# Splitting the routed experts' weights early, through DRAM, and building the one-hot tables in eight pieces

## The reference, cut to what matters

```python
x = x + L0_ffn(L0_cond(x, ...))        # attention (16 heads, cosine), then relu^2 MLP 256->1024->256, then a 5-step spiking count
x = x + L1_ffn(L1_cond(x, ...))        # attention (16 heads), then a transformer block with a mixture of experts
# inside L1_ffn, for the normed token t:
probs  = softmax(t @ Wr.T)             # 8 experts; the best 2 by probs + bias are taken
routed = sum_k w_k * (silu(t @ eW1[e_k].T) * (t @ eW3[e_k].T)) @ eW2[e_k].T
shared = (silu(t @ sW1.T) * (t @ sW3.T)) @ sW2.T
```

## Time and profile before

| what | value |
|---|---|
| median of three runs | 1526.59 us (1524.34 to 1528.87) |
| the profiled execution, its span | 1527.73 us, 1526.0 us |
| PE busy | 1349.5 us (88%) |
| DVE, ACT, POOL busy | 1127.1 (74%), 893.8 (59%), 795.6 us (52%) |
| mean granted TensorE clock | 0.957 of full |

### The profile page before, as it was taken

The page is one execution under the profiler, slowest core; times in us unless marked ns, Lnnn a source line. Parts: engine busy times, 40 slices in busy tenths (PEclk is TensorE's granted clock), DMA queues, the critical chain, the costliest instruction groups (busy, mean ns, idle before and its releaser), DMA issues.

```text
span 1526.0 us, 43298 instructions
## 1 busy us (share of the span) xinstructions
PE 1349.5 (88%) x15534; PEld 1178.9 (77%) x15535; DVE 1127.1 (74%) x2218; ACT 893.8 (59%) x2229; POOL 795.6 (52%) x838
## 2 busy tenths in 40 slices
PE   1889999999759999979999999768998867999993
PEld 0778988889648999868888888547787756888883
DVE  4488888888844556689999999748886797545457
ACT  1457767667527666746665666437786544545556
POOL 1256656665505545555555555358884023777740
PEclk9899999999979999999999999979997989999997
DMA  7210000000011000000000000110003203233318
GB/s 203 33 36 8 9 8 8 10 8 9 33 30 53 1 0 0 1 9 9 9 7 9 9 9 8 26 48 15 14 14 111 74 1 121 93 101 99 96 43 331
DMA packets 82391, 65.09 MB, mean 43 GB/s; under 512 B 50734, under 2 KB 76081, under 8 KB 81202
## 3 DMA queue, kind: packets, MB, share of 16 engines
q1 hardware_dynamic: 75314, 44.98, 10.3%
q0 software_dynamic: 6912, 17.84, 3.7%
HBM read 39.18 MB, written 18.35 MB: 38 GB/s over the span
## 4 chain that ended last, share of the span: by engine, by line
PE 75%; DVE 10%; issue 6%; ACT 5%; POOL 2%; SPq 1%; DMA 1%; DVEq 0%; ACTq 0%; POOLq 0%
PE psW L1968 12%; PE psQ L1889 12%; PE psQ L2261 8%; PE psW L2240 4%; PE psS L1950 4%; PE psS L1993 4%; PE psT L1926 3%; PE psQ L2062 3%; PE psW L2050 3%; PE psM L2050 3%; PE psS L2062 3%; PE psM L1937 2%; PE psT L2229 1%; PE psM L1907 1%; PE psT L2248 1%
## 5 line engine op out<-in xcount | busy, mean ns | idle before, releaser
L732 POOL TENSOR_TENSOR pn<-ex,rden 128x1024 f32<-128x1024 f32 x64 | 144.0, 2250 | 245.3 <-PE psT L1926 240.7
L1889 PEld LDWEIGHTS psQ<-xT,wq 128*128 128x128 f32 x1536 | 201.1, 200 | 46.0 <-issue 24.1
L1968 PE MATMUL psW<-wout,oT 128*128 128x256 f32 x1536 | 210.3, 292 | 16.4 <-ACT oT L963 14.4
L1889 PE MATMUL psQ<-xT,wq 128*128 128x256 f32 x1536 | 220.9, 297 | 1.5 <-ACT cur L1044 1.5
L1968 PEld LDWEIGHTS psW<-wout,oT 128*128 128x128 f32 x1536 | 195.3, 194 | 29.3 <-ACT oT L963 24.0
L2261 PE MATMUL psQ<-W,exT 128*128 (+1 forms) x624 | 173.8, 414 | 0.0
L777 POOL TENSOR_TENSOR hT<-hf,hT 128x512 fp32r<-128x512 f32 x64 | 84.4, 1318 | 99.9 <-ACT hT L1040 99.9
L2261 PEld LDWEIGHTS psQ<-W,exT 128*128 128x128 f32 x624 | 112.2, 193 | 19.2
L2240 PE MATMUL psW<-W,ehT 128*128 (+1 forms) x624 | 103.4, 303 | 8.3 <-DVE ehT L1803 8.2
L1347 DVE SCALAR_TENSOR_TENSOR oT<-psS,nvcol,oT 128x512 fp32r<-128x512 f32 x128 | 89.7, 740 | 23.8 <-ACT oT L963 23.2
L1320 DVE TENSOR_TENSOR ex<-ex,m 128x1040 f32<-128x1040 f32 x64 | 103.6, 1619 | 2.2
(11 more groups left out here) (310 smaller groups left out, 3477.3 us busy)
## 6 DMA issues: line engine op xcount, KB each, us to landing
both<-results SPq DMA_DIRECT2D x8, 1024.0 KB, 13.3
raw_w<-W SPq DMA_DIRECT2D x27, 256.0 KB, 4.2
vv<-vp SPq DMA_DIRECT2D x256, 16.0 KB, 1.8
xf<-xf_all SPq DMA_DIRECT2D x4, 1024.0 KB
out<-X SPq DMA_DIRECT2D x8, 512.0 KB, 5.0
X<-x SPq DMA_DIRECT2D x1, 3584.0 KB, 14.3
raw_q<-Wq SPq DMA_DIRECT2D x2, 1024.0 KB, 6.0
bvv<-v_all SPq DMA_DIRECT2D x128, 16.0 KB, 1.8
```

The source lines that it names most:

```text
L732: nc.gpsimd.tensor_tensor(pn[:], ex[t % 2][:, :, 0:S], rden[:].unsqueeze(2).to_broadcast([P, H, S]), ALU.mult).then_inc(sem("t_pn"), 1)
L1889: mm = nc.tensor.matmul(psQ[:, cc, h * QT:h * QT + QT], wq[w][:, k, c * P:c * P + P], xT[g % 2][u][:, k, :], start=(k == 0 and j == 0), st ...
L1968: mm = nc.tensor.matmul(psW[:, 0:D], oT[u][:, c, :], wout[w][:, c, :], start=(u == 0 and c == 0 and w == 0), stop=(u == 1 and c == CH - 1))
```

## The change

The weights of the eight routed experts are no longer split in the routing stage. In each of the eight groups of the feed-forward, one expert is loaded into a small buffer, its three pieces are split at f = 1, 3 and 5 (the hi copy on ScalarE, the lo on VectorE, one pair of buffers for both), and SyncE stores hi and lo into a DRAM tensor. Each expert later comes into its slot by one load of 1.57 MB. Only the shared expert is still split in place, at steps -4 to -2. The one-hot tables are made in eight pieces of 8 columns through two buffers each, so they take one slot instead of four; TensorE multiplies a piece in each of steps 13 to 20. Ranking, scan with tile ends, and places move to steps 9, 10 and 11, the tables' product ends at step 20, and the index tables move from step 20 to 21. Three semaphores are merged into others.

```diff
-PROBS, CHOICE, RANK, SCAN, ENDS, PLACES, HOT, SLOTS, TABLES = 5, 6, 10, 11, 12, 13, 14, 19, 20
+PROBS, CHOICE, RANK, SCAN, PLACES, HOT, SLOTS, TABLES = 5, 6, 9, 10, 11, 12, 19, 21
+PIECES = 8
-SPLIT_STEP = ([-4, -3, -2] + [0, 1, 2] + [3, 4, 5] + [10, 10, 10] + [SLOTS] * 3 + [21] * 4 + [22] * 4 + [23] * 4)
+SPLIT_STEP = (-4, -3, -2)
+PRE = 3 * E
+PRE_F = (1, 3, 5)
...
+        pre_raw = sb("ffn_work", "pre_raw", [P, EW], F32)
+        pre_w = [sb("ffn_work", f"pre_w{i}", [P, 2 * D], F32R) for i in range(2)]
+        w_dram = nc.dram_tensor("split_w", (E, P, 2, EW), F32, kind="Internal").ap()
...   SyncE, after the fside loads of layer 1 and before its attention
+            sp.dma_start(g2col[:], a["g2"].rearrange("(k p) -> p k", p=P), ...).then_inc(sem("e_first"), 16)
+            for g in range(E):
+                reach(sp, sem("e_wlo"), 3 * g)
+                load_expert(g + 1, pre_raw[:])
+                for part in range(3):
+                    sp.wait_ge(sem("e_wlo"), 3 * g + part + 1)
+                    third = slice(part * 2 * D, part * 2 * D + 2 * D)
+                    for w in range(2):
+                        sp.dma_start(w_dram[g, :, w, third], pre_w[w][:].bitcast(F32)).then_inc(sem("w_stored"), 16)
...   SyncE, later
+            load_expert(0, raw_w[:, SHARED_SLOT, 1, :])
+            sp.wait_ge(sem("w_stored"), 32 * PRE)
+            load_split(1)
...                                            # at the end of the block: load_split(2)
-            for p in (3, EP - 1):
-                load_expert(p, (p + 1) % EP, sem("e_rest"))
-            sp.wait_ge(sem("r_ranked"), 2)
-            sp.wait_ge(sem("r_given"), 3)
-            for p in range(4, EP - 1):
-                load_expert(p, p + 1, sem("e_last"))
+            for p in (3, 5, 6, 7, 8):
+                load_split(p)
+            sp.wait_ge(sem("r_ranked"), 1 + PIECES)
+            load_split(4)
...   ScalarE, in ffn() after ffn_hi() of f = 1, 3, 5
+            def presplit_hi(g, part):
+                act.wait_ge(sem("e_first"), 48 * g + 64)
+                reach(act, sem("w_stored"), 96 * g + 32 * part)
+                nc.scalar.activation(pre_w[0][:], pre_raw[:, part * 2 * D:part * 2 * D + 2 * D], ACT.Copy, scale=...).then_inc(sem("e_whi"), 1)
...   VectorE, in ffn() at f = 1, 3, 5
+            def presplit_lo(g, part):
+                dve.wait_ge(sem("e_whi"), 3 * g + part + 1)
+                ...pre_w[1] = raw * gain - pre_w[0]....then_inc(sem("e_wlo"), 1)
...   VectorE, in first_half()
+                if HOT < i <= HOT + PIECES:
+                    one_hot_rows(i - HOT - 1)
+                if HOT <= i < HOT + PIECES:
+                    one_hot_tiles(i - HOT)
...   ScalarE, in first_half()
+                if HOT <= i < HOT + PIECES:
+                    c = i - HOT
+                    act.wait_ge(sem("r_hot"), c + 1)
+                    nc.scalar.activation(hot_part[c % 2][:], hot_tile[c % 2][:], ACT.Copy, scale=iota_part[:, 0:1]).then_inc(sem("r_part"), 1)
...   TensorE, in first_half()
-                elif i == SLOTS:
-                    pe.wait_ge(sem("r_hots"), 4 + 2 + 1)
+                elif HOT < i <= HOT + PIECES:
+                    c = i - HOT - 1
+                    for ready in ("r_hots", "r_part", "r_number"):
+                        pe.wait_ge(sem(ready), c + 1)
                     ... 16 of the 128 matmuls each time
...   TensorE, the first routed up product (t == FIRST)
-                        pe.wait_ge(sem("e_wlo"), 3 * EP if t else 3)
+                        pe.wait_ge(sem("e_last"), 16 * E)
```

More of the change, by code:

```diff
@@ L62 @@
 WHOLE = 1.5 * 2.0 ** 23
-ORDER = (SHARED_SLOT, 2, 3, 4, 0, 5, 6, 7, 8)
 NEG = -1e30
@@ L400, in build @@
         hot_at = w_at + 5 * 12 * K
-        hot_row = nc.alloc_sbuf_tensor_at("hot_row", [P, TOP_K * TILES, P], BF16, offset=hot_at)
-        hot_tile, hot_part, hot_number = (nc.alloc_sbuf_tensor_at(f"hot_{n}", [P, TOP_K * TILES, ROUTED], BF16, offset=hot_at + 16 * K + 9216 * i)
-                                          for i, n in enumerate(("tile", "part", "number")))
+        region("hot", 12 * K, at=hot_at)
+        HQ = TOP_K * TILES // PIECES
+        hot_row = [sb("hot", f"hot_row{i}", [P, HQ, P], BF16) for i in range(2)]
+        hot_tile, hot_part, hot_number = ([sb("hot", f"hot_{n}{i}", [P, HQ, ROUTED], BF16) for i in range(2)] for n in ("tile", "part", "number"))
         n_tiles = sb("route", "n_tiles", [P, E], F32)
@@ L420, in build @@
         idx = [sb("tile", f"idx{i}", [P, 1], I32) for i in range(BUFS)]
-        by_end = nc.alloc_sbuf_tensor_at("by_end", [1, ROUTED, E], F32, offset=hot_at + 16 * K + 9216 * 3)
+        by_end = nc.alloc_sbuf_tensor_at("by_end", [1, ROUTED, E], F32, offset=place["bias"][0] - 4 * K)
         slot_f = [sb("route", f"slot_f{i}", [1, ROUTED], F32) for i in range(2)]
@@ L859, in store_result @@
                                              oob_is_err=False).then_inc(sem(f"e_stored{m}"), 16)
-            pool.wait_ge(sem("r_hot"), 1)
-            nc.gpsimd.tensor_tensor(hot_number[:], hot_tile[:], number[:].unsqueeze(2).to_broadcast([P, TOP_K * TILES, ROUTED]),
-                                    ALU.mult).then_inc(sem("r_hots"), 1)
+            for c in range(PIECES):
+                pool.wait_ge(sem("r_hot"), c + 1)
+                nc.gpsimd.tensor_tensor(hot_number[c % 2][:], hot_tile[c % 2][:],
+                                        number[:, c * HQ:c * HQ + HQ].unsqueeze(2).to_broadcast([P, HQ, ROUTED]), ALU.mult).then_inc(sem("r_number"), 1)
             pool.wait_ge(sem("xf_stored"), 16 * 5)
@@ L1051, in ffn @@
                     ffn_hi(FC * g + f, f % 2)
+                    if f in PRE_F:
+                        presplit_hi(g, PRE_F.index(f))
                     if last and f == 2:
@@ L1518, in ffn @@
                         ffn_normalise(g + 1)
+                    if f in PRE_F:
+                        presplit_lo(g, PRE_F.index(f))
                     if last and f == 4:
@@ L1621, in _, with split_shared @@
             dve.wait_ge(sem("xf_stored"), 16)
-            def split_expert(n, part):
-                slot = ORDER[n]
-                dve.wait_ge(sem("e_whi"), 3 * n + part + 1)
+            def split_shared(part):
+                dve.wait_ge(sem("e_whi"), PRE + part + 1)
                 third = slice(part * 2 * D, part * 2 * D + 2 * D)
-                hi = W[:, slot, 0, third].bitcast(F32)
-                lo, raw = W[:, slot, 1, third], raw_w[:, slot, 1, third]
+                hi = W[:, SHARED_SLOT, 0, third].bitcast(F32)
+                lo, raw = W[:, SHARED_SLOT, 1, third], raw_w[:, SHARED_SLOT, 1, third]
                 if part < KD:
@@ L1830, in first_half @@
                     top_weights()
-                for piece in range(3 * EP):
-                    if SPLIT_STEP[piece] == i:
-                        split_expert(piece // 3, piece % 3)
+                if HOT < i <= HOT + PIECES:
+                    one_hot_rows(i - HOT - 1)
+                if HOT <= i < HOT + PIECES:
+                    one_hot_tiles(i - HOT)
+                if i == SLOTS:
+                    tile_slots()
+                if i in SPLIT_STEP:
+                    split_shared(SPLIT_STEP.index(i))
             def merged(i):
@@ L2273, in first_half @@
                     mm.then_inc(sem("r_ranked"), 1)
-                elif i == SLOTS:
-                    pe.wait_ge(sem("r_hots"), 4 + 2 + 1)
+                elif HOT < i <= HOT + PIECES:
+                    c = i - HOT - 1
+                    for ready in ("r_hots", "r_part", "r_number"):
+                        pe.wait_ge(sem(ready), c + 1)
                     for b, what in enumerate((hot_part, hot_number)):
-                        for q in range(TOP_K * TILES):
-                            mm = nc.tensor.matmul(psS[:, b, 0:ROUTED], hot_row[:, q, :], what[:, q, :], start=(q == 0), stop=(q == TOP_K * TILES - 1))
+                        for q in range(HQ):
+                            mm = nc.tensor.matmul(psS[:, b, 0:ROUTED], hot_row[c % 2][:, q, :], what[c % 2][:, q, :],
+                                                  start=(c == 0 and q == 0), stop=(c == PIECES - 1 and q == HQ - 1))
                     mm.then_inc(sem("r_ranked"), 1)
```

103 lines of the change are left out of this document (48 added, 55 removed).

## The result

The changed kernel took 1532.84 us (median of 11 runs, 1529.61 to 1538.12) beside 1528.19 for the kernel before (11 runs, 1522.67 to 1530.19): 1.0039 times as long, 95% interval 1.0028 to 1.0051. That is slower by 0.39%, little more than the 0.3% that the prediction took for the smallest change one can tell; 1521.1 was forecast. The spans of the two profiled executions, 1532.0 and 1526.0, differ by 6.0 us, and the stages add up to that. A group of the feed-forward runs from its first transposes to those of the next group; `cur` is the tile that ScalarE copies out when the last group is done; the last step is step 103, a tile of the shared expert.

A forecast was written before the change was run, and what follows sets the result against it. TensorE was taken as the bound, with time to gain only where it waits, before the routed tiles. -12.1 + 4.5 + 1.0 + 1.1 = -5.5 took 1527.73 to 1522.2 us, median 1521.1; 8-in-10 range 1512 to 1532.

The forecast's parts named there:

- Last group: Feed-forward's last group: ScalarE has no idle, three copies 2.0 less 0.9 of gaps; cost 1.1 us, bounds 0 and 2.
- rival A: Middle groups: stores' round trip makes ScalarE wait before second and third hi; 15 us, 1536; chance 0.20.
- Start of the feed-forward: First group: ScalarE waits 5.4 us for the first expert load; cost 4.5 with lowered clock, bounds 2.5 and 8.
- Rival B: Feed-forward's start: first weights land late and the clock drops, cost 8 instead of 4.5, 1525; chance 0.12.
- Middle groups: Feed-forward's middle groups: copies and store waits nearly hidden, 0.2 a group; cost 1.0 us in all, bounds 0 and 15.
- Routing stage: Up to step 25: splits go, tables made in pieces at 4.2 us a step; gain 12.1 us, bounds 17 and 3.
- C: Routing stage: pieces pipeline better, 3.2 us a step instead of 4.2; 7.5 us less, 1513.5; chance 0.17.
- D: Steps 13 to 20: each waits for a piece, TensorE at 1.2 GHz, 5.5 us a step; 9 more, 1530; chance 0.05.

The follow-up runs named there:

- after_again: The changed kernel itself, unaltered, measured again: ratio 1.0057 to the kernel before.
- third_part: third_late, with ScalarE multiplying its piece one step later in the routing stage: ratio 0.9955 to the kernel before.
- third_prod: third_part, with TensorE's product of a piece one step later too and index tables at step 22: ratio 0.9908 to the kernel before.
- no_presplit: The changed kernel without the split and its ScalarE and VectorE pieces; raw weights stored in both halves, loads and stores kept: ratio 0.9979 to the kernel before.
- third_late_b: third_late run once more, beside a trace of the kernel before: ratio 0.9930 to the kernel before.
- third_late: Changed kernel; expert 1 loaded before layer 1's weights, last group's first lo before norm_second, expert 8's third piece between last norm's halves: ratio 0.9989 to kernel before.

## Why the prediction was wrong

The prediction's sum came to 1522.2 for the profiled execution; the changed kernel's took 1533.7. Of these 11.5 us the last group makes 9.2, the first 1.4 and the routing stage 1.3; the middle groups give 0.9 back, and 0.5 is the drift of the two stages that the change does not touch.

*The step that failed* is "Last group": cost 1.1, bounds 0 and 2; it measured 10.3 and 6.8 in two traces. It added up only ScalarE's busy time (three copies, 2.0) and took the group's order from the middle groups. Three things were missing. First, the one pair of buffers: the prediction followed "the next hi waits for the last piece's two stores" through a middle group only. In the last group VectorE's lo piece stands behind norm_second, which waits 4.7 us for GpSimd's rstd, and behind two spike counts; that wait cost nothing before, and no row of the prediction shows it; it became a wait of ScalarE and through it of TensorE. Secondly, the third piece stands in front of wout's 1.90 us and relu(6). Moving the first lo piece took 2.0 off (38.1 to 36.1), moving the third piece 3.6 more (36.1 to 32.5), and 1.2 is left, the lateness of relu(6) that was forecast. In all of these a part is not the wait but TensorE's clock behind it. Thirdly, the exclusion of GpSimd by VectorE, with 3.5 more in one of two traces. The prediction used it as a reason for rival A, where it cost nothing, and did not ask for it where the last down product waits for GpSimd. That it is VectorE's chain which holds GpSimd there rests on the overlap of the rows and on the two lengths of one kernel's operations; no run took the chain away alone.

*Start of the feed-forward*: right in mechanism and place, 5.9 and 6.8 in two traces instead of 4.5. Both terms were too small. Counted from the first transposes, relu(2) came 7.3 and 7.4 us later than before, where 6.1 was worked out, mainly because SyncE took 3.8 and 3.6 us to issue the g2 column and the three loads, not 4 times 0.47. Down(2) came 5.2 and 5.3 later instead of 4.0. And TensorE's products behind the wait cost 0.75 and 1.4 more by their clock, where 0.5 was allowed (mean clock of the group 0.78 and 0.76, 0.84 before). Rival B's 8 did not come.

*Middle groups*: 0.1 instead of 1.0. The stores landed in 2.3 us, below the 2.9 that was the best row of before; ScalarE's waits for stores sum to 10.9, 4.8 of it in the last group, the other 12 being 0.5 each on average. VectorE's lo pieces did grow, the first two of an expert to a median of 0.95 and at most 1.28 us from 0.74, which fits the exclusion by GpSimd, and that too stayed hidden. So rival A is refuted for the middle groups, where it was placed. In the last group the wait that it named did come, in front of the second piece, but because VectorE was late, not because the stores took long. The estimate from the Trainium skill (DMA: Bandwidth & Descriptors, Anatomy of one DMA), 3.2 for the pair, was nearer than the 5.0 of the queued output stores, though the Trainium skill fits it to DMAs that GpSimd issues and these are SyncE's. The Trainium skill's warning about writes to HBM finds no example in these stores.

*Routing stage*: 10.8 instead of 12.1, and only 10.3 up to step 25, for which the 12.1 was worked out. The spacing is 4.33 where 4.2 was worked out, from the order hot_row and hot_tile on VectorE, ScalarE's piece, Silu, VectorE's last operations. That makes the pieces 0.9 longer in all. The last piece with the body of step 21 took 5.4 instead of 3.9, because TensorE had stood for 2.38 us and ran at 0.72 of its clock there, and the first gathered rows landed 0.4 later than allowed; against that, 1.1 had been gained more than forecast before the pieces began. (after_again gained 0.6 less than the first trace in steps 6 to 25.) third_part and third_prod bear out that account, as taking ScalarE's piece out of the chain and then TensorE's product lets the spacing fall to VectorE's 3.1, "if engines only had to be busy". Rivals C (3.2) and D (5.5) did not come. No load was waited for, and the last one landed in 6.3 us, about the 7 allowed; no_presplit, whose ScalarE has none of the copies, has the same 80.4.

With 1.2 in the last group for 10.3 and 0.5 in the first for 5.9, 1532.84 becomes 1518.3; third_late_b is that kernel, 1518.19 beside 1529.5. The range ended at 1532, and 1532.84 lies 0.84 outside it, less than the 3.5 by which the last group differs between the two traces. The chance of 0.20 for a slower kernel was tied to the middle groups alone, and the loss came from another place.

## What to carry to other kernels

When work is spread evenly over a loop, follow it separately through the first and the last iteration: that is where the operand is not there yet, and where other work has been placed. A wait that costs nothing is not free room: whatever is queued behind it inherits it. Where engines pass a piece on inside one step, give the consumer the piece of the step before; each hand-over taken out of the chain showed at once (4.33, 3.94, 3.11).

## What the runs showed of the hardware

The same kernels took 1583 to 1587 us in some measurements and 1527 to 1530 in others. The difference lies in the routed tiles alone: third_late needs 252.6 us from step 27 to its last step where it took 1580.0, and 197.9 where it took 1518.2; the stages before, from the start of the feed-forward to step 25, agree to 1.3 us each. Windows of third_late, then of third_late_b:

```profile
1300.00:1400.00 100.00, 78.02 (x456) 63.81 (x454) 36.31 (x143) 36.08 (x112) 56.51 (x57) 1.00 0.23 75
```

```profile
1300.00:1400.00 100.00, 99.05 (x615) 85.00 (x614) 50.04 (x190) 50.99 (x154) 75.93 (x78) 1.00 0.31 99
```

The clock is the same. Each trace from the measurements of 1583 to 1587 us has 5.0 to 9.7 us between steps 26 and 27, the others 2.5 to 2.6. From 1285 to 1480 ScalarE's result waits 48.7 us in third_late, in 21 waits, for a releaser that the view of waits calls remote, none of the engines; in third_late_b it never does; that fits scatters which finish later, since a result buffer is free only when its scatter is done, but no run measured them. There, too, an earlier start is partly given back: the same kernel was 2.8 us faster than the kernel before as third_late and 11.3 as third_late_b, and no_presplit, which reaches step 25 100.8 us after step 0 instead of 109.5 and loses nothing in the feed-forward, was only 0.21% faster. What makes the routed tiles slow in one measurement and not in another stays open; the chip alone does not, since the record has chip 12 for a measurement of either kind.
